# A two-layer graph network on one core: index tables, carry rows, vector features and the third pass laid out anew

## The chip, the cores and the metric

The kernel runs on 1 core of one Trainium2 chip. The metric is device time in microseconds (us), the median of several runs.

## The reference

There are 100,000 nodes with 160 features each (64 scalars and 32 three-vectors), and 25,000 edges, sorted by destination, with 4 and 8 attributes. Two layers run one after the other, each on the layer-normed and clipped rows:

```python
h = jnp.maximum(_layernorm(x), 0.0)
# layer 0, with attr = node_vec1, ys = edge_attr_4[:, :1], yv = edge_attr_4[:, 1:]
weight = silu(edge_attr_8 @ fc_w1 / sqrt(8)) @ fc_w2 / sqrt(64)          # E x 192
f_s, f_v = linear(h) * attr ; gs, gv = f_s[src], f_v[src]
m0a = gs * ys * w1_                      ; m0b = sum(gv * yv) * INV3 * w4_
m1a = gs[..., None] * yv * w2_[..., None] ; m1b = gv * ys * w3_
mid = segment_sum([m0a, m0b, m1a, m1b], dst) / 4
angle = 0.1 * mid_s @ lin3_w / sqrt(96) * attr
x = x + cos(angle) * (h @ sc_w * attr) + sin(angle) * (mid @ lin2_w * attr)
# layer 1: s, v of the new h at src; e0, e1 the edge attributes
out0 = C0 * (s * e0 @ W1 + dot(v, e1) * INV3 @ W2)
out1 = C1 * ((s @ W3) * e1 * INV3 + (v * e0) @ W4 * INV3 + cross(v, e1) @ W5 * INV6)
x = x + relu(segment_sum([out0, out1], dst) @ [Ws, Wv])
```

## The kernel before

All arithmetic is float32. Edges are cut into T = 196 tiles of 128, four tiles to a quad (Q = 49 quads); nodes are cut into U = 98 units of 1024 rows (8 rows a partition). Each engine runs its own list, written out by hand, with semaphores between them; there is no planner. The stages, in order:

- **Prologue.** SyncE (SP) loads the index tables, weights and first node rows. VectorE (DVE) makes from them the gather index `t_gat`, the scatter index `t_put` (far out of bounds where the next edge has the same destination) and keys `f_key`, and SP stores these in DRAM tables `src_tab`, `dst_tab`, `put_tab`, `key_tab`, `row_tab` (lines 409 to 418). Behind these stores in SP's list come the 13 groups of the edge network: load `scalars_t` (`net_load`, line 427), two products on TensorE (PE, line 1037), Silu on ScalarE (ACT, line 803), store `hid_tab` (line 433).
- **Pass 1.** A step is one dense unit and two edge tiles; two steps are a quad. Dense part: moments, centring (`hb`, `hr`), transposes (line 976), products (`dense_mm`, lines 981, 982), `dense_x1` (DVE, line 1358), second norm (`nmr`, line 1211), `dense_h1` (ACT, line 774, four instructions for half a unit), and the sum `yo` on GpSimd (POOL, line 649). Edge part: gather rows (`p1_gather`), transposes, products (lines 981, 982, 1066), `p1_source` (ACT, line 824, scales the product into `g_e`), `p1_features` in three DVE parts (lines 1423, 1428, 1432), transposes (line 1090), message parts (lines 1052 to 1055), message (line 1411), and the running segment sum: `same` selector times messages plus `carry` selector times the tile before (lines 1078, 1080), copied out by `p1_total` (ACT, line 832). One PE turn ("slot") is: `dense_mm`, `p1_feat_t`, `p1_parts`, `p1_source`, `p1_sum`, then `dense_tr`. `dense_tr` waits for `e_tot`, the signal of `p1_total`, as the sum and the transposed rest share PSUM bank 1. ACT's turn is `p1_feat_t`, `p1_rest`, `p1_source`, `p1_total`, then the dense copies and `dense_h1`.
- **Pass 2.** For each quad, rows at the destinations are gathered (POOL, line 606), the first layer is finished with the sums, and h of layer 1 is scattered (POOL, line 612).
- **Pass 3.** For each tile n: gather (line 738), `p3_features` (DVE, lines 1686, 1688: the row scaled by e0, and 288 products), four transposes, copy `fT` (ACT, line 951), `p3_parts` (five products, lines 1166 to 1170), `p3_message` and `p3_message_sum` (DVE, lines 1697, 1703), `p3_sum` (PE), `p3_total` (ACT), `p3_out` (DVE, line 1712), scatter (line 612). PE's slot n is `p3_tr(n-1)`, `p3_sum(n-4)`, `p3_parts(n-2)`. The selectors are built per quad from `q_row`, a row of 512 destinations that SP broadcasts to 128 partitions, in SP's list behind the load of `i_put`, which waits for the scatters of the quad two before.

Of the kernel before, what the change touches and what calls it, by code (L numbers as in the profile page):

```python
# [34 lines left out]
W_WS, W_WVK, W_WV, W_WVA, W_WVB, W_END = 2211, 2275, 2371, 2403, 2499, 2595  # L35
# [39 lines left out]
def gnn_kernel(nc, xa, src, dst, number, edges_in, scalars_in, scalars_t_in, wpack, out):  # L75
# [34 lines left out]
    row_q = row_tab.rearrange("(q c) p -> q (c p)", c=GQ)  # L110
    ed_q = edges.rearrange("p (q c) f -> q p (c f)", c=GQ)
# [9 lines left out]
    with ExitStack() as ctx:  # L121
# [32 lines left out]
        f_key = sb("f_key", [P, Q, 2 * GQ])  # L154
        t_row = two("t_row", [P, P])
# [25 lines left out]
        inv1, inv2 = four("inv1", [P, GD]), two("inv2", [P, GD])  # L181
# [11 lines left out]
        i_put = two("i_put", [P, GQ], i32)  # L193
        q_key = two("q_key", [P, 2 * GQ])
        q_row = two("q_row", [P, GQ * P])
# [10 lines left out]
        g_e = two("g_e", [P, D])  # L206
        feat = two("feat", [P, 512])
        fT = two("fT", [P, 512])
# [4 lines left out]
        n_sct = [t[0:GQ * SW, 0:CH] for t in yo]  # L213
# [55 lines left out]
        d_mm = sem("dense_product_done")  # L269
        d_scl = sem("dense_scale_ready")  # L270
# [21 lines left out]
        e_fm = sem("p1_feature_step")  # L292
# [40 lines left out]
        m_ft = sem("p3_features_ready")  # L333
        m_ss = sem("p3_scalars_copied")
# [32 lines left out]
        def _(sp):  # L367
            sp.dma_start(t_src[:, :], src).then_inc(s_tab_in, 16)
            sp.dma_start(t_dst[:, :], dst).then_inc(s_tab_in, 16)
            sp.dma_start(wp[:, :], wpack).then_inc(s_w, 16)  # L370

            sp.wait_ge(s_fill, 2)
            sp.dma_start(t_next[0:P - 1, :], dst[1:P, :]).then_inc(s_tab_in, 16)
            sp.dma_start(t_next[P - 1:P, 0:T - 1], dst[0:1, 1:T]).then_inc(s_tab_in, 16)
            sp.dma_start(t_prev[P - 1:P, 1:T], dst[P - 1:P, 0:T - 1]).then_inc(s_tab_in, 16)
# [3 lines left out]
            sp.dma_start(scalars_t.rearrange("q f p -> (q f) p"), scalars_t_in.rearrange("q f p -> (q f) p")).then_inc(s_rows, 16)  # L379
            sp.wait_ge(s_flag, 1)  # L380
            with sp.If(sp.value_load(unsorted[0:1, 0:1], min_val=0, max_val=1) > 0):

                sp.wait_ge(s_rows, 32)
# [12 lines left out]
                sp.dma_start(t_src[:, :], src_sorted).then_inc(k_tab, 16)  # L396
# [9 lines left out]
                sp.wait_ge(k_sct2, 16 * T)  # L406

            sp.wait_ge(s_tabc, 6)
            sp.dma_start(src_tab.rearrange("q p c -> p q c"), t_src[:, :].rearrange("p (q c) -> p q c", c=GQ)).then_inc(s_tab_out, 16)
            sp.dma_start(dst_tab.rearrange("q p c -> p q c"), t_gat[:, :].rearrange("p (q c) -> p q c", c=GQ)).then_inc(s_tab_out, 16)  # L410
            sp.dma_start(put_tab.rearrange("q p c -> p q c"), t_put[:, :].rearrange("p (q c) -> p q c", c=GQ)).then_inc(s_tab_out, 16)
            sp.dma_start(key_tab.rearrange("q p c -> p q c"), f_key[:, :, :]).then_inc(s_tab_out, 16)
            sp.wait_ge(s_rowsb, 1)
            sp.dma_start(row_tab[0:TA, :], t_row[0][0:TA, :]).then_inc(s_tab_out, 16)
# [1409 lines left out]
```

## Time and profile before

| | before |
|---|---|
| median of 3 runs | 2458.61 us (2458.08 to 2460.48) |
| the profiled execution's own time | 2459.89 us |
| its span, first to last instruction | 2458.1 us |
| prologue, to the end of the edge network | 0 to 111.9 us |
| pass 1 | 112 to about 1372 us |
| pass 2 | about 1376 to 1906 us |
| pass 3 | about 1907 to 2458 us |
| mean granted TensorE clock | 0.883 of full |

Busy time alone says little here: each stage has another engine that sets its pace, so each is read for itself. "Idle before" is the time an engine sat unused ahead of an instruction, with what released it. Instructions on one engine overlap at their edges, so start-to-start distances are what a turn costs.

### The profile page before, as it was taken

What the parts mean: (1) busy time and instruction counts of PE and PEld (TensorE: products, weight loads), DVE (VectorE), ACT (ScalarE), POOL (GpSimd) and SP (SyncE); (2) the same over time, 40 slices, a digit from 0 to 9 for tenths busy, and PEclk for the clock granted to TensorE, in tenths of its full rate; (3) what the DMA queues carried; (4) which work ended last, traced back from release to release, by engine and by line L of the source; (5) the groups of instructions that cost most, each with busy time, mean ns of one, the idle gap of its engine ahead of it and who ended that gap; (6) DMA issues with size and microseconds to landing.
All of it is one profiled execution on the core that took longest, in us unless ns stands there. A gap on an engine that the chain in (4) does not pass through costs nothing.

```text
span 2458.1 us, 51427 instructions
## 1 busy us (share of the span) xinstructions
PE 1824.8 (74%) x12730; PEld 1696.7 (69%) x12730; DVE 1873.4 (76%) x5982; ACT 1296.0 (53%) x3409; POOL 1477.5 (60%) x1432
## 2 busy tenths in 40 slices
PE   0788888888888888888888554544543788898887
PEld 0287778777787777877777544444443788888887
DVE  2099999999999999999999676666666566665564
ACT  0256666666666666666666555555555333333332
POOL 1045455554545555455553677777777777777776
PEclk9999999999999999999999755555555899998999
DMA  9445555555555555555555534334433334444443
GB/s 85 145 139 186 196 206 202 196 188 195 200 201 203 190 195 191 201 205 194 195 184 185 172 108 118 114 116 123 117 117 117 94 105 111 115 111 110 113 115 85
DMA packets 236558, 377.35 MB, mean 154 GB/s; under 512 B 116353, under 2 KB 146108, under 8 KB 236364
## 3 DMA queue, kind: packets, MB, share of 16 engines
q1 hardware_dynamic: 189484, 302.66, 39.1%
q0 software_dynamic: 47040, 74.31, 11.2%
q8 instruction: 12, 0.20, 0.0%
q14 instruction: 22, 0.18, 0.0%
HBM read 183.27 MB, written 201.21 MB: 156 GB/s over the span
## 4 chain that ended last, share of the span: by engine, by line
PE 33%; issue 17%; DVE 14%; ACT 12%; DMA 12%; POOL 6%; SPq 4%; ACTq 1%; DVEq 1%; POOLq 0%
ACT h L774 6%; PE bank L981 5%; DMA q_row<-row_tab 4%; PE bank L976 4%; DMA x_all<-in_xa,i_dst 3%; DVE st L1207 3%; POOL h_all L612 3%; PE bank L1090 3%; PE bank L982 3%; PE bank L1066 2%; DMA out<-yo,i_put 2%; POOL x_all L606 2%; PE bank L1158 2%; ACT h L889 2%; ACT tot L832 2%
## 5 line engine op out<-in xcount | busy, mean ns | idle before, releaser
L649 POOL TENSOR_TENSOR yo<-x,h 128x640 f32<-128x640 f32 x196 | 303.9, 1551 | 506.2 <-ACT h L774 504.9
L981 PE MATMUL bank<-wp,hT 128*128 128x160 f32 x1568 | 376.3, 322 | 0.0
L774 ACT ACTIVATE h<-x,nmr,inv 128x160 f32<-128x160 f32 x784 | 342.2, 514 | 1.5 <-DVE nmr L1211 1.5
L606 POOL DMA_INDIRECT x_e<-in_xa,i_src x192 | 210.8, 1098 | 161.1 <-issue 78.3
L981 PE MATMUL bank<-wp,eT 128*128 128x160 f32 x784 | 263.0, 428 | 51.2 <-ACT eR L897 43.7
L982 PE MATMUL bank<-wp,hR 128*128 128x64 f32 x1568 | 259.4, 247 | 0.0
L1358 DVE SCALAR_TENSOR_TENSOR x<-bank,scl,x_all 128x160 f32<-128x160 f32 x784 | 254.7, 365 | 5.1 <-PE bank L982 1.8
L982 PEld LDWEIGHTS bank<-wp,hR 128*128 128x128 f32 x1568 | 255.5, 190 | 0.0
L612 POOL DMA_INDIRECT out<-yo,i_put x196 | 209.7, 1070 | 74.3 <-issue 41.0
L612 POOL DMA_INDIRECT h_all<-h,i_put x196 | 217.4, 1109 | 59.8 <-issue 58.9
L976 PE MATMUL bank<-ident,h_e 128*128 128x128 f32 x392 | 83.9, 353 | 215.8 <-DVE hr_e L1527 215.4
L981 PEld LDWEIGHTS bank<-wp,hT 128*128 128x128 f32 x1568 | 237.7, 192 | 2.1
L738 POOL DMA_INDIRECT h<-h_all,i_src x196 | 200.2, 1022 | 61.5 <-issue 44.5
L606 POOL DMA_INDIRECT x_all<-in_xa,i_dst x196 | 192.4, 981 | 59.6 <-issue 57.8
L795 ACT ACTIVATE hT<-bank 128x512 f32<-128x512 f32 x196 | 117.0, 597 | 208.2 <-PE bank L977 208.2
L1207 DVE BATCH_NORM_STATS2 st<-x 128x6 f32<-128x320 f32 x490 | 217.9, 484 | 0.0
L976 PEld LDWEIGHTS bank<-ident,h_e 128*128 128x128 f32 x392 | 58.2, 185 | 224.7 <-DVE hr_e L1527 207.1
L981 PEld LDWEIGHTS bank<-wp,eT 128*128 128x128 f32 x784 | 163.5, 258 | 70.7 <-issue 38.2
L976 PE MATMUL bank<-ident,hb 128*128 128x128 f32 x784 | 124.3, 281 | 110.3 <-ACT tot L832 110.3
L946 ACT ACTIVATE tot<-bank 128x160 f32<-128x160 f32 x196 | 59.0, 301 | 267.9 <-PE bank L1181 264.0
L1158 PE MATMUL bank<-ident,feat 128*128 128x128 f32 x784 | 129.0, 290 | 93.2 <-DVE feat L1688 92.5
L976 PEld LDWEIGHTS bank<-ident,hb 128*128 128x128 f32 x784 | 83.1, 141 | 152.5 <-issue 137.6
(161 smaller groups left out, 5508.3 us busy)
## 6 DMA issues: line engine op xcount, KB each, us to landing
x_all<-in_xa SPq DMA_DIRECT2D x98, 644.0 KB, 5.0
h_all<-h SPq DMA_DIRECT2D x98, 640.0 KB, 3.0
out<-yo SPq DMA_DIRECT2D x98, 640.0 KB, 3.3
q_row<-row_tab SPq DMA_DIRECT2D x98, 256.0 KB
sum_tab<-tot SPq DMA_DIRECT2D x49, 322.0 KB, 4.2
y_tab<-yo SPq DMA_DIRECT2D x49, 320.0 KB
x<-y_tab SPq DMA_DIRECT2D x49, 320.0 KB
cv<-sum_tab SPq DMA_DIRECT2D x25, 322.0 KB, 3.2
```

Of the source, the lines that this page charges most:

```text
L606: nc.gpsimd.indirect_dma_start(into[:, t * width:(t + 1) * width], None, rows, bass.IndirectOffsetOnAxis(ap=index[:, t:t + 1], axis=0)).th ...
L612: nc.gpsimd.indirect_dma_start(rows, bass.IndirectOffsetOnAxis(ap=index[:, t:t + 1], axis=0), tile, None, bounds_check=N - 1, oob_is_err=F ...
L649: nc.gpsimd.tensor_tensor(yo[j][:, a:b], x1[j][:, a:b], h1[j][:, a:b], ALU.add).then_inc(d_y, 1)
L738: nc.gpsimd.indirect_dma_start(h1[j][:, t * D:(t + 1) * D], None, h1_all, bass.IndirectOffsetOnAxis(ap=i_src[j][:, t:t + 1], axis=0)).then ...
L774: ins = nc.scalar.activation(h1[j][:, k * D:(k + 1) * D], x1[j][:, k * D:(k + 1) * D], ACT.Relu, bias=nmr2[j][:, k:k + 1], scale=inv2[j][: ...
L795: nc.scalar.activation(hT[h][:, :], bank[0][:, :], ACT.Relu)
L976: nc.tensor.transpose(ps_main[:, t * P:(t + 1) * P], main[:, t * P:(t + 1) * P], ident[:, :])
L981: nc.tensor.matmul(dst_ps, main[:, t * P:(t + 1) * P], wp[:, w:w + D], start=True, stop=False)
L982: return nc.tensor.matmul(dst_ps[:, 0:DS], rest[:, :], wp[:, w + D + t * DS:w + D + (t + 1) * DS], start=False, stop=True)
L1158: ins = nc.tensor.transpose(bank[n.mod(2)][:, c * P:(c + 1) * P], feat[n.mod(2)][:, c * P:(c + 1) * P], ident[:, :])
L1207: return V.bn_stats(st[:, 2 * pair:2 * pair + 2, :].rearrange("p g k -> p (g k)"), two_rows[:, 0:D, :])
L1358: ins = V.scalar_tensor_tensor(x1[j][:, k * D:(k + 1) * D], bank[2 + pair % 2][:, k % 2 * D:(k % 2 + 1) * D], scl1[u.mod(4)][:, k:k + 1], ...
```

## The change

- **Index copies.** The four DRAM tables of indices and keys are gone. DVE copies four columns of `t_src`, `t_gat`, `t_put` from SBUF into `i_src`, `i_dst`, `i_put` some quads ahead (`index_copy`, with an address from a register); `q_key` gives way to columns of `f_dst`. `i_put` has four buffers in place of two.
- **Carry rows.** The carry selector has only its last row non-zero. A table `carry_tab` of these rows is made once (a compare of each row with the tile's predecessor), and per quad SP loads one row of 512 into partition 127 of `carry[j]`. The second `is_equal` of each quad on DVE is gone, in pass 1 and in pass 3. `row_tab` is now a copy of an input, int32.
- **Prologue.** The table stores and the transposes for rows are gone; loads are in another order; four network groups are loaded ahead in place of one; message weights take 11 products in place of 16.
- **Scale through PSUM.** `dense_inverse` writes its 8 columns into PSUM bank 2, `dense_scale` reads them there; both sit inside `dense_x1` of the unit before. PE's first product of a unit waits for the scale.
- **Vector features of pass 1.** `p1_source` on ACT writes, beside the scaled 160 columns, three more pieces of 32 columns with a stride of three, each scaled by attribute and scale (`scly`, made by one new POOL instruction per quad). `p1_features` has two DVE parts; the in-place product of line 1432 is gone. `p1_tables` moves to the even step.
- **Pass 3 in three chunks.** ACT scales the row by e0. DVE makes the 288 products into `prod`, and after `p3_message` the dot (a reduction of 96 to 32) and the cross product (64 and 32 columns). The features are 352 wide in place of 512: three transposes, four products, and a copy of `fT` in two ACT instructions. `q_row` is loaded a quad earlier, by itself.

The core of the diff:

```diff
@@ SP, pass 1 @@
             def step(v, last=False, laststore=False):
-                if v.mod(2) == 0 and (q + 1).within(Q):
-                    p1_load(q + 1)
+                if v.mod(2) == 0 and q.within(Q):
+                    p1_tables(q)
                 if v.mod(2) == 1 and q.within(Q):
-                    p1_tables(q)
+                    p1_carry(q)
                     p1_hidden(q)
+            def p1_carry(q):
+                j = q.mod(2)
+                wait(sp, e_seg, q.times(GQ, -GQ))
+                sp.dma_start(carry[j][P - 1:P, :], carry_q[q.times(1)].unsqueeze(0)).then_inc(e_ca[j], 16)
@@ SP, prologue @@
-            sp.wait_ge(s_tabc, 6)
-            sp.dma_start(src_tab.rearrange("q p c -> p q c"), ...).then_inc(s_tab_out, 16)
...
-            sp.dma_start(key_tab.rearrange("q p c -> p q c"), f_key[:, :, :]).then_inc(s_tab_out, 16)
...
+            sp.wait_ge(s_rows, 48)
-            net_load(0)
+            for g in range(4):
+                net_load(g)
+            sp.wait_ge(s_car, 1)
+            sp.dma_start(carry_tab[0:TA, :], c_row[0][0:TA, :]).then_inc(s_car_out, 16)
@@ SP, pass 3 @@
+            def p3_rows(q):
+                j = q.mod(2)
+                wait(sp, m_sc, q.times(1, -1))
+                sp.dma_start(q_row[j][:, :], row_q[q.times(1)].partition_broadcast(P)).then_inc(m_rw[j], 16)
+            def p3_step(q, ahead=True):
+                if ahead:
+                    p3_rows(q + 1)
+                p3_edges(q)
+                p3_y(q)
+                p3_carry(q)
@@ POOL @@
             def p1_scale(q):
...
+                pool.wait_ge(e_scl, q.times(4, 3))
+                pool.wait_ge(e_tb[j], q.over(2, 32, 32))
+                nc.gpsimd.tensor_tensor(scly[j][:, :].rearrange("p (t i) -> p t i", i=3), bc_last(scl_e[j][:, :], 3),
+                                        x3(q_ed[j], EW, GQ)[:, :, 1:4], ALU.mult).then_inc(e_scl, 1)
@@ ACT @@
             def p1_source(n):
-                nc.scalar.activation(g_e[n.mod(2)][:, :], bank[5 + n.mod(2)][:, 0:D], ACT.Copy,
-                                     scale=scl_e[j][:, t:t + 1]).then_inc(e_gg, 1)
+                g, b = g_e[n.mod(2)], bank[5 + n.mod(2)]
+                nc.scalar.activation(g[:, 0:D], b[:, 0:D], ACT.Copy, scale=scl_e[j][:, t:t + 1])
+                for c in range(3):
+                    ins = nc.scalar.activation(g[:, D + c:D + DV:3], b[:, DS + c:D:3], ACT.Copy,
+                                               scale=scly[j][:, 3 * t + c:3 * t + c + 1])
+                ins.then_inc(e_gg, 1)
             def p3_scalars(n):
-                nc.scalar.activation(feat[n.mod(2)][:, 448:512], h1[j][:, t * D:t * D + DS], ACT.Copy).then_inc(m_ss, 1)
+                nc.scalar.activation(f[:, 0:D], h, ACT.Copy, scale=ed(j, t, 0, 1))
+                nc.scalar.activation(f[:, 288:352], h[:, 0:DS], ACT.Copy).then_inc(m_ss, 1)
@@ PE, pass 3 @@
-                for c in range(4):
-                    ins = nc.tensor.transpose(bank[n.mod(2)][:, c * P:(c + 1) * P], ...)
+                for c in range(2):
+                    nc.tensor.transpose(b[:, c * P:(c + 1) * P], f[:, c * P:(c + 1) * P], ident[:, :])
+                nc.tensor.transpose(b[0:DV, 2 * P:3 * P], f[:, 256:352], ident[:, :]).then_inc(m_ftr, 1)
@@ DVE @@
+            def index_copy(into, table, q, signal):
+                V.tensor_copy(into[:, :], table[:, bass.ds(q.times(GQ), GQ)]).then_inc(signal, 1)
             def dense_inverse(u):
-                V.reciprocal(inv1[j][:, :], sd1[j][:, :]).then_inc(d_scl, 1)
+                V.reciprocal(bank[2][:, 2 * D:2 * D + GD], sd1[u.mod(4)][:, :]).then_inc(d_inv, 1)
             def p1_selectors(q):
-                selector(same, q.mod(2), 0)
-                selector(carry, q.mod(2), 1).then_inc(e_sc, 1)
+                selector(q).then_inc(e_sc, 1)
             def p1_features(n, part):
-                else:
-                    v.wait_ge(e_fm, n.times(1, 1))
-                    V.tensor_tensor(f[:, 224:320]..., f[:, 224:320]..., bc_mid(ed(j, t, 1, 4), DU), ALU.mult).then_inc(e_ft, 1)
             def p3_slot(n):
                 if n.within(T):
                     p3_features(n)
                 if (n - 2).within(T):
                     p3_message(n - 2)
+                if n.within(T):
+                    p3_dot_cross(n)
                 if (n - 4).within(T):
                     p3_out(n - 4)
...
-                if n.mod(4) == 0 and n.within(T):
-                    selector(carry, n.c // GQ % 2, 1).then_inc(m_sc, 1)
```

## Rows read from the trace of the kernel before

**Rows 1.** The page's slices of PE: the span in 40 equal parts.

```profile
PE   0788888888888888888888554544543788898887
```

**Rows 2.** Busy time in four stretches: PE, PEld, DVE, ACT, POOL, clock, DMA.

```profile
60.00:114.00 54.00, 45.82 (x57) 15.96 (x57) 0.00 (x0) 15.27 (x27) 0.00 (x0) 1.00 0.44 136
600.00:700.00 100.00, 83.56 (x645) 78.50 (x645) 94.68 (x271) 64.44 (x181) 52.85 (x52) 1.00 0.58 200
1700.00:1800.00 100.00, 49.29 (x193) 43.78 (x192) 67.43 (x290) 53.79 (x101) 77.75 (x74) 0.55 0.40 118
2100.00:2200.00 100.00, 86.09 (x651) 84.87 (x651) 58.58 (x198) 33.84 (x109) 76.68 (x75) 0.93 0.43 113
```

**Rows 3.** Timeline of the prologue, SP's queue and PE.

```profile
18.75 10.62 SPq L410 DMA_DIRECT2D dst_tab<-t_gat  x1
...
63.98 7.16 PE L1037 MATMUL bank<-yo,wp 32*128 32x512 f32 x8 [44.74 <-DMA yo<-scalars_t]
...
110.66 1.22 PE L1037 MATMUL bank<-yo,wp 32*128 32x128 f32 x4 [0.44 <-DMA yo<-scalars_t]
```

**Rows 4.** DMA issues: KB each, median us to landing.

```profile
scalars_t<-in_scalars_t_in SPq DMA_DIRECT2D x1, 784.0 KB, 9.7
```

**Rows 5.** Waits, 200 to 1300 us: total us, times, longest.

```profile
PE bank L976 <- ACT tot L832: 98.4, 173, 0.6
...
PE bank L1090 <- DVE feat L1432: 36.3, 43, 0.8
```

**Rows 6.** The copy at line 811, once a quad, quads 2 to 48.

```profile
L811 ACT ACTIVATE eT<-bank x47: 597/597/598, 160.5 to 1333.1; 128x512 f32<-128x512 f32 x47
```

**Rows 7.** Timeline of one turn of pass 1, ACT and PE.

```profile
608.08 0.39 ACT L824 ACTIVATE g_e<-bank,scl_e 128x160 f32<-128x160 f32 x1 [0.65 <-PE bank L1066]
608.62 0.30 ACT L832 ACTIVATE tot<-bank 128x161 f32<-128x161 f32 x1 [0.15 <-PE bank L1080]
...
609.18 0.63 PE L976 MATMUL bank<-ident,hb 128*128 128x128 f32 x4 [0.60 <-ACT tot L832]
```

**Rows 8.** ACT's groups by shape, 200 to 1300 us: busy, mean ns.

```profile
L774 ACT ACTIVATE h<-x,nmr,inv 128x160 f32<-128x160 f32 x691 | 301.7, 514 | 0.0
...
L824 ACT ACTIVATE g_e<-bank,scl_e 128x160 f32<-128x160 f32 x173 | 68.1, 394 | 112.8 <-PE bank L1066 112.8
L832 ACT ACTIVATE tot<-bank 128x161 f32<-128x161 f32 x173 | 52.8, 305 | 20.2 <-PE bank L1080 18.0
...
L817 ACT ACTIVATE xr<-bank 128x65 f32<-128x65 f32 x172 | 38.5, 224 | 18.9 <-PE bank L1055 15.4
```

**Rows 9.** Timeline, four instructions of line 774 in a row.

```profile
605.00 1.75 ACT L774 ACTIVATE h<-x,nmr,inv 128x160 f32<-128x160 f32 x4
```

**Rows 10.** Timeline, DVE beside POOL in pass 1.

```profile
606.91 1.54 POOL L649 TENSOR_TENSOR yo<-x,h 128x640 f32<-128x640 f32 x1 [4.23 <-ACT h L774]
...
607.35 1.13 DVE L1348 TENSOR_TENSOR scl<-inv,x_all 128x8 f32<-128x8 f32 x1
```

**Rows 11.** POOL's groups in pass 3 (1950 to 2430 us).

```profile
L612 POOL DMA_INDIRECT out<-yo,i_put x177 | 189.2, 1069 | 58.5 <-issue 32.4 <-DVE feat L1688 10.5 <-ACT feat L941 6.1
L738 POOL DMA_INDIRECT h<-h_all,i_src x176 | 180.1, 1023 | 53.6 <-issue 39.9 <-DVE yo L1712 8.2 <-ACT feat L941 5.5
```

**Rows 12.** Timeline of one turn of pass 3, PE and DVE.

```profile
2200.09 0.60 PE L1158 MATMUL bank<-ident,feat 128*128 128x128 f32 x4
...
2202.04 0.39 PE L1170 MATMUL bank<-msg1d,fT 128*128 128x96 f32 x2
...
2202.26 0.60 PE L1158 MATMUL bank<-ident,feat 128*128 128x128 f32 x4
...
2202.46 0.26 DVE L1697 TENSOR_TENSOR xr<-bank,q_ed 128x96 f32<-128x96 f32 x1 [0.75 <-PE bank L1170]
```

**Rows 13.** A DVE instruction on 4 columns, in pass 2.

```profile
L1571 DVE TENSOR_SCALAR trig<-trig 128x4 f32<-128x4 f32 x43 | 6.8, 158 | 0.0
```

**Rows 14.** A DVE group of pass 3, the carry selector (1950 to 2430 us).

```profile
L1384 DVE TENSOR_TENSOR carry<-q_row,q_key 128x512 f32<-128x512 f32 x44 | 29.9, 680 | 0.0
```

More of the change, by code:

```diff
@@ L192, in gnn_kernel @@
         i_dst = four("i_dst", [P, GQ], i32)
-        i_put = two("i_put", [P, GQ], i32)
-        q_key = two("q_key", [P, 2 * GQ])
-        q_row = two("q_row", [P, GQ * P])
+        scly = two("scly", [P, 3 * GQ])
+        i_put = four("i_put", [P, GQ], i32)
+        q_row = two("q_row", [P, GQ * P], i32)
         q_ed = two("q_ed", [P, GQ * EW])
@@ L205, in gnn_kernel @@
         eR = two("eR", [P, P])
[L206 removed]
+        g_e = two("g_e", [P, D + DV])
         feat = two("feat", [P, 512])
[L208 removed]
+        fT = two("fT", [P, 384])
+        prod = two("prod", [P, 3 * DV])
         xr = two("xr", [P, CW])
@@ L253, in gnn_kernel @@
         k_tab = sem("sorted_tables_loaded")
+        n_row = 64 if T > P else 32
         block = ctx.enter_context(nc.Block())
-        n_in = sem2("net_scalars_loaded")
+        n_in = [sem(f"net_scalars_loaded{i}") for i in range(4)]
         n_mm = sem("net_products_done")
@@ L509, in _ @@
                 step(At(0, v), last=v == U - 1)
-            for q in range(4):
-                p2_index(At(0, q))
             step(At(0, U + 3), laststore=True)
@@ L519, in p2_sums @@
                 sp.dma_start(cv[q.mod(4)], sum_tab[q.times(1)]).then_inc(r_cv[q.mod(4)], 16)
-            def p2_put(q):
-                j = q.mod(2)
-                wait(sp, r_put[j], q.over(2, 64))
-                sp.dma_start(i_put[j][:, :], put_tab[q.times(1)]).then_inc(r_px[j], 16)
             def p2_store(q):
@@ L632, in _ @@
                     pool.sem_inc(k_go, 1)
-                pool.wait_ge(k_tab, 80)
+                pool.wait_ge(k_tab, 64 + n_row)
+            for j in range(2):
+                nc.gpsimd.memset(carry[j][:, :], 0.0)
+            nc.gpsimd.memset(tot[1][:, :], 0.0).then_inc(s_cz, 1)
             def p1_gather(q):
                 j = q.mod(2)
-                pool.wait_ge(e_ix[j], q.over(2, 16, 16))
+                pool.wait_ge(e_ix, q.times(1, 1))
                 wait(pool, e_cen, q.times(1, -1))
+                wait(pool, e_scl, q.times(4, -4))
                 gather(xa, x_e[j], XW, i_src[j], e_g[j])
@@ L783, in dense_root1 @@
                 act.wait_ge(d_ln1, u.times(1, 1))
-                wait(act, d_scl, u.times(2, -7))
+                wait(act, d_inv, u.times(1, -3))
                 root(sd1[u.mod(4)], st1[u.mod(4)], GD, d_sq1)
@@ L1016, in dense_mm @@
                 for k in range(GQ):
+                    if h == 0 and k == 0:
+                        pe.wait_ge(d_scl, u.times(1, 1))
                     if k % 2 == 0:
@@ L1379, in dense_shift2, with selector @@
                 shift_of(nmr2[j], st2[j], inv2[j], GD, d_nmr)
-            def selector(into, j, key):
-                return V.tensor_tensor(x3(into[j], P, GQ), x3(q_row[j], P, GQ),
-                                       bc_last(q_key[j][:, key * GQ:(key + 1) * GQ], P), ALU.is_equal)
+            def selector(q):
+                j = q.mod(2)
+                key = f_dst[:, bass.ds(q.times(GQ), GQ)]
+                return V.tensor_tensor(x3(same[j], P, GQ), x3(q_row[j], P, GQ), bc_last(key, P), ALU.is_equal)
+            def index_copy(into, table, q, signal):
+                V.tensor_copy(into[:, :], table[:, bass.ds(q.times(GQ), GQ)]).then_inc(signal, 1)
             def p1_stats(q):
@@ L1486, in step @@
                     p1_message(s1 - 2)
-                if tile:
-                    p1_features(s1, 2)
                 if odd:
                     p1_selectors(q1)
+            v.wait_ge(s_src_in, 16)
+            for q in range(2):
+                index_copy(i_src[q], t_src, At(0, q, 2), e_ix)
             dense_stats(At(0, 0))
@@ L1624, in p2_step @@
                     p2_stats(q)
+                if (q + 3).within(Q):
+                    index_copy(i_dst[(q + 3).mod(4)], t_gat, q + 3, r_ix)
+                if c:
+                    wait(v, r_put[q.mod(2)], (q - 2).over(2, 64, -64))
+                    index_copy(i_put[(q - 2).mod(4)], t_put, q - 2, r_px)
                 if b:
@@ L1659, in p2_step @@
                     p2_angle(q, 7)
+            for q in range(3):
+                index_copy(i_dst[q], t_gat, At(0, q), r_ix)
             v.wait_ge(d_y, 2 * U)
```

361 lines of the change are left out of this document (174 added, 187 removed).

## The prediction

> **What bounds the kernel now.** I read the page's slices first, then the stages' busy times, then in each stage the wait that ends last. The slices show four stages: PE is 80% busy in passes 1 and 3 and half idle in pass 2 [rows 1]. The table of stretches names a different engine each time [rows 2]. From 60 to 114 us nothing but PE and ACT works; in pass 1 DVE is at 94.7%, in pass 2 POOL is at 78%, in pass 3 POOL is at 77% and PE at 86%.
>
> *Prologue.* SP stores tables until 63.98 us, where the first network product starts; the last one ends at 110.66 + 1.22 = 111.9 [rows 3]. Eight products (two groups) take 7.16 us, and 12 groups took 46.68 us, so a pair costs 7.78, of which 0.6 is waiting for a load.
>
> *Pass 1.* The quad's period is (1333.1 − 160.5)/46 = 25.49 us [rows 6]. DVE's 94.7% tempts one to call it the bound, but the waits show a loop through PE: every tile PE stands 0.57 us (98.4/173) for ACT's `tot`, and only once a quad 0.84 us (36.3/43) for DVE's features [rows 5]. Without the second the quad would be 24.65. The tail of the turn is in the timeline: `g_e` starts at 608.08, `tot` 0.54 later, PE goes on 0.56 after that [rows 7]. So what lengthens `g_e` on ACT lengthens PE's turn.
>
> *Pass 2.* PE idles half of the time and runs at 0.55 of its clock [rows 2]; POOL's indirect DMAs, eight a quad, set the pace.
>
> *Pass 3.* POOL's two groups and their idle time fill 189.2 + 180.1 + 58.5 + 53.6 = 481 of 480 us: 2.73 a tile, 10.9 a quad, most of the idle time being issue [rows 11]. PE's own turn is 2202.26 − 2200.09 = 2.17 us [rows 12]; it catches up and waits again for selectors.
>
> **The change, part by part** (profiled execution's own time 2459.9, 1.3 above the median).
>
> *Prologue, −43.* What remains before the network is the load of `scalars_t`, 9.7 us [rows 4], which landed ahead of the first store at 18.75 [rows 3]. With small transfers more (about 2) and a group load (about 3) the first product starts near 25. With four groups loaded ahead the loads vanish: 12 groups at 3.58 plus 1.22 is 44.2, end at 69, against 111.9: −43. Bounds: start at 20 gives −48; the old 7.78 a pair, or weights that come late, −35. The carry rows' compare, the clearing on POOL and the shorter weight products lie beside these 44 us, where DVE and POOL are idle [rows 2]; uncovered they would cost under 5.
>
> *Pass 1, vector features, +23.5.* ACT gains three pieces of 32 columns a tile. Two sizes of copy from PSUM, 161 columns in 0.305 and 65 in 0.224, give 0.84 ns a column; the scaled 160 took 0.394, 0.09 more than the copy [rows 8]. So a scaled piece of 32 is 0.224 − 0.028 + 0.09 = 0.285. ACT overlaps neighbours: four instructions of 0.514 took 1.75, a spacing of 0.41 for each, so 0.10 is hidden [rows 8, 9]. A piece then adds 0.18. ACT reaches `tot` after 0.29 + 3 × 0.18 = 0.84 in place of 0.54 (today 0.15 of that is waiting for PE): +0.30 a turn. The quad: 24.65 + 4 × 0.305 + 0.10 of leftover DVE waits = 25.97, +0.48, times 49 = +23.5. Bounds: pieces at 0.12 add 0.11 a turn, −15; at 0.285 with no overlap 0.60, +82.
>
> DVE loses one feature product a tile and one selector a quad, and gains the index copy, which I put between 0.158, DVE's 4-column instruction [rows 13], and 0.29: 1.3 to 3 us less a quad. That opens slack but no time, save the 0.84 wait counted above. The reciprocal into PSUM and the scale inside `dense_x1` take their old durations; the scale took 1.13 us for 8 columns while POOL was in its sum [rows 10]. With one SBUF operand it may shed that stall, which now runs into `hb` instead or disappears. Both lie in DVE's slack. `dense_mm` waits for the scale, but the scale precedes it by most of a step; if late, PE's first product of a unit waits. POOL's new 12-column product waits for the edge table and queues ahead of the later sums; POOL is 53% busy [rows 2], so nothing.
>
> Here the Trainium skill speaks against the index copies ("SBUF — State Buffer", § SBUF: two separate sides): a DVE copy of float32 within SBUF takes the port pair that GpSimd needs to write its DMA descriptors, and one side waits whole. By it 98 copies in passes 2 and 3 would cost up to about 0.2 us each, +20 by my estimate; the 1.13 us row agrees that the two engines meet, but no row here shows a copy beside an indirect DMA.
>
> *Index copies, pass 2, +3.* SP's loads were hidden, so removing them gives nothing; two copies a quad on DVE (67% busy) sit beside POOL, the bound. At 0.03 net each, 49 × 2 × 0.03 = +3; bounds 0 and, if each held POOL for 0.2 us, +20. The four `i_put` buffers remove no wait that shows.
>
> *Pass 3, +5.* The carry selector, 0.68 us on DVE a quad [rows 14], goes; beside POOL's DMAs I count 0.4 of it as gain, so POOL would want 10.5 a quad. But dot and cross come after the message, which waits for PE's parts. Today the transposes start 0.17 before the last product ends (2202.26 against 2202.43) [rows 12]. Afterwards they start behind message 0.26, reduction (as the 96-column message) 0.26, two subtractions between 0.158 and 0.26, 0.22 and 0.18 [rows 12, 13]: 0.92 less three overlaps of 0.10 (taken as ACT's) plus 0.07 of signals = 0.69 to 0.71. That is +0.88 on PE's turn. One transpose fewer gives 0.11, the dropped product 0.22 (2202.26 − 2202.04): 2.17 + 0.88 − 0.33 = 2.72, 10.9 a quad. PE's loop and POOL's then lie side by side, with little room to catch up: 11.0, +0.1 × 49 = +5. ACT's scaled row and split copy lie in its 34% of work [rows 2]. `q_row` loaded a quad earlier takes a wait away that would otherwise hold PE, already inside the 10.9. Bounds: POOL alone at 10.5, −20; cross at 1.05 of chain, +0.8 a quad, +40.
>
> Sum: 2459.9 − 43 + 23.5 + 3 + 5 = 2448.4; less 1.3, **2447 us**.
>
> **Rivals.** *B, the pieces are cheap.* If DVE's load was what made PE late (94.7% speaks for it, the waits against it), its 1.3 to 3 us less a quad count: the quad falls to 25.0 and pass 3 to 10.7: −43 − 24 − 10 + 3 = **2385**.
>
> *C, the other side: ACT's three pieces cost more than the prologue gives.* Place: between `g_e` and `tot`, every tile. The prologue and the rest give 35, 49 × (24.75 + 4e) − 49 × 25.49 = 35 at e = 0.363 a turn, a piece of 0.20. I work with 0.18; strided reads and writes speak for more. Without overlap, 0.605: +82 in place of +23.5, **2506**. The Trainium skill ("ScalarE: Activation LUTs", § What ACT_TABLE_LOAD costs) gives a fixed part, 0.833 ns a column and 93 ns for a pointer scale; my estimate from it is 0.213 a piece, e = 0.39, about 2463; its slope agrees with the 0.84 of the rows.
>
> *D, PE's clock.* Passes 2 and 3 show 0.55 at 49% busy and 0.93 at 86% [rows 2]. A turn of 2.72 with about 0.9 idle lies between. At 0.8 some 0.4 us a tile is added, +80: **2525**.
>
> *E, the change doesn't do what it says:* the network still starts late because its loads queue behind the carry rows or weights; then +20 to +40 on the forecast, 2480.
>
> **How the numbers follow.** The forecast has 0.48; its own range is 2425 to 2470 (bounds −15 on the pieces, +20 on the copies). B 0.19, C 0.21, D 0.07, E 0.05. About 0.2% of the median, 5 us, is what a measurement can tell. Of the forecast 0.33 is faster, 0.09 same, 0.06 slower; B is faster; of C 0.03 is same and 0.18 slower, of D and E 0.01 and 0.11. Faster 0.52, same 0.13, slower 0.35. The range of 8 in 10 cuts a tenth at either end, inside B's and C's spread: 2400 to 2498.
>
> **What would show it.** First network product near 25 us and last end near 69, else the prologue's step is wrong. The `eT` copy's period 26.0 (B: 25.0, C: above 26.2); `g_e` to `tot` 0.84; PE's wait for `tot` 0.87 a tile and none for DVE's features. Pass 2 at its old length within 5 us. In pass 3 PE idle before the transposes with DVE's cross as releaser, POOL no longer filled. Wrong would be: POOL's indirect DMAs longer than 1.07 and 1.02, or a granted clock in pass 3 under 0.9.

## Result and the profile after

The changed kernel takes 2485.35 us (median of 4 runs, 2481.81 to 2490.46) against 2458.35 for the kernel before on the same chip: ratio 1.0124, 95% interval 1.0101 to 1.0147. It is 27 us slower. The forecast, 2447, had the sign wrong; the range, 2400 to 2498, holds the time. The profiled execution took 2483.92 with a span of 2482.1.

First the stages. Each has an instruction whose first start marks its beginning: the first `eT` copy (pass 1), the first gather into `x_all` (pass 2) and the first gather into `h` (pass 3). These are rows of single lines; after the colon stand the shortest, median and longest duration in ns, then first and last start in us. Before:

```profile
L811 ACT ACTIVATE eT<-bank x49: 597/597/598, 113.6 to 1333.1; 128x512 f32<-128x512 f32 x49
L606 POOL DMA_INDIRECT x_all<-in_xa,i_dst x196: 942/967/1575, 1376.7 to 1878.2; - x196
L738 POOL DMA_INDIRECT h<-h_all,i_src x196: 942/975/1472, 1907.8 to 2428.6; - x196
```

The changed kernel, and its `tot` copy of pass 3, one a tile:

```profile
L816 ACT ACTIVATE eT<-bank x49: 597/597/597, 67.7 to 1312.3; 128x512 f32<-128x512 f32 x49
L604 POOL DMA_INDIRECT x_all<-in_xa,i_dst x196: 942/951/1638, 1357.2 to 1867.4; - x196
L743 POOL DMA_INDIRECT h<-h_all,i_src x196: 942/975/1399, 1897.5 to 2449.7; - x196
L958 ACT ACTIVATE tot<-bank x196: 303/304/308, 1915.3 to 2472.4; 128x160 f32<-128x160 f32 x196
```

Differences of these starts, and of the spans' ends, give:

| stage | before, us | after, us | measured | forecast |
|---|---|---|---|---|
| prologue (to the first `eT`) | 113.6 | 67.7 | −45.9 | −43 |
| pass 1 | 1263.1 | 1289.5 | +26.4 | +23.5 |
| pass 2 | 531.1 | 540.3 | +9.2 | +3 |
| pass 3 (to the end of the span) | 550.3 | 584.6 | +34.3 | +5 |
| sum | 2458.1 | 2482.1 | +24.0 | −11.5 |

So 29 of the 36 us by which the sum is off are in pass 3, 6 in pass 2. The same four stretches as in [rows 2] (stretch, length, then PE, PEld, DVE, ACT, POOL, clock, DMA share, GB/s):

```profile
60.00:114.00 54.00, 42.42 (x262) 36.62 (x261) 34.11 (x100) 28.19 (x86) 19.00 (x24) 1.00 0.39 125
600.00:700.00 100.00, 82.61 (x636) 77.42 (x636) 91.79 (x250) 69.65 (x224) 53.96 (x55) 1.00 0.56 194
1700.00:1800.00 100.00, 49.45 (x194) 44.28 (x194) 66.85 (x300) 53.70 (x102) 77.75 (x73) 0.53 0.38 116
2100.00:2200.00 100.00, 72.48 (x525) 66.40 (x525) 59.67 (x272) 42.04 (x175) 72.98 (x71) 1.00 0.39 109
```

The first stretch now holds work of pass 1 as well. Of the other three the last differs most: in pass 3 PE fell from 86% to 72% busy and POOL from 77% to 73%. No engine is full there, which points to a loop of waits. The prologue in the timeline, against [rows 3]: the first network product starts at 23.76, and all 52 run on without a load wait, to 65.94.

```profile
23.76 42.18 PE L1042 MATMUL bank<-yo,wp 32*128 32x512 f32 x52 [10.02 <-DMA yo<-scalars_t]
```

One turn of pass 1, ACT and PE, against [rows 7]:

```profile
605.01 0.32 ACT L841 ACTIVATE tot<-bank 128x161 f32<-128x161 f32 x1
...
605.58 0.63 PE L989 MATMUL bank<-ident,hb 128*128 128x128 f32 x4 [0.86 <-ACT tot L841]
...
611.84 0.40 ACT L830 ACTIVATE g_e<-bank,scl_e 128x160 f32<-128x160 f32 x1 [0.65 <-PE bank L1071]
612.13 0.65 ACT L832 ACTIVATE g_e<-bank,scly 128x32 f32<-128x32 f32 x3
612.64 0.33 ACT L841 ACTIVATE tot<-bank 128x161 f32<-128x161 f32 x1
```

`g_e` to `tot` is 0.80 (was 0.54), each piece adding (612.64 − 612.13)/3 = 0.17. PE's wait for `tot` is 0.88 a tile (was 0.57), as the waits of 200 to 1300 us say (total, times, longest):

```profile
PE bank L989 <- ACT tot L841: 149.1, 169, 1.0
```

PE's wait for DVE's features, 0.84 a quad in [rows 5], is gone from PE's list. The quad is (1312.3 − 139.9)/45 = 26.05 us, forecast 25.97.

One turn of pass 3, PE and DVE, against [rows 12]:

```profile
2209.51 0.44 PE L1168 MATMUL bank<-ident,feat 128*128 128x128 f32 x2 [0.80 <-DVE feat L1708]
...
2211.21 0.36 PE L1178 MATMUL bank<-msg1c,fT 96*128 96x96 f32 x2
...
2211.60 0.26 DVE L1715 TENSOR_TENSOR xr<-bank,q_ed 128x96 f32<-128x96 f32 x1 [1.32 <-PE bank L1178]
2211.78 0.24 DVE L1706 TENSOR_REDUCE feat<-prod 128x32 f32<-128x96 f32 x1
...
2212.10 0.19 DVE L1708 TENSOR_TENSOR feat<-prod 128x32 f32<-128x32 f32 x1
...
2212.35 0.44 PE L1168 MATMUL bank<-ident,feat 128*128 128x128 f32 x2 [0.78 <-DVE feat L1708]
```

This is a closed circle: products end at 2211.57, the message starts at 2211.60, the reduction and two subtractions follow, and the transposes start at 2212.35, 0.78 after the products' end. All that time PE stands. DVE stood 1.32 us just before it.

### The profile page after: what moved, and what is told of

It is laid out like the page before. It is cut to its first block and busy times, and to the rows that moved or that the text cites. A ratio compares the mean times of both kernels' runs of the same rounds, so it can differ in the third digit from the quotient of the medians.

```text
span 2482.1 us, 51663 instructions
## 1 busy us (share of the span) xinstructions
PE 1775.0 (72%) x12130; PEld 1619.9 (65%) x12130; DVE 1873.2 (75%) x6324; ACT 1426.8 (57%) x4389; POOL 1505.6 (61%) x1485
## 5 line engine op out<-in xcount | busy, mean ns | idle before, releaser
L651 POOL TENSOR_TENSOR yo<-x,h 128x640 f32<-128x640 f32 x196 | 326.7, 1667 | 499.5 <-ACT h L779 498.3
L604 POOL DMA_INDIRECT x_e<-in_xa,i_src x196 | 204.4, 1043 | 98.5 <-issue 70.0
L610 POOL DMA_INDIRECT h_all<-h,i_put x196 | 224.5, 1145 | 59.8 <-issue 59.2
L743 POOL DMA_INDIRECT h<-h_all,i_src x196 | 194.1, 991 | 61.7 <-issue 57.6
L1715 DVE TENSOR_TENSOR xr<-bank,q_ed 128x96 f32<-128x96 f32 x196 | 50.4, 257 | 233.8 <-PE bank L1178 233.8
L1168 PE MATMUL bank<-ident,feat 128*128 128x128 f32 x392 | 87.0, 304 | 180.3 <-DVE feat L1708 153.8
```

The source lines that it names most:

```text
L604: nc.gpsimd.indirect_dma_start(into[:, t * width:(t + 1) * width], None, rows, bass.IndirectOffsetOnAxis(ap=index[:, t:t + 1], axis=0)).th ...
L610: nc.gpsimd.indirect_dma_start(rows, bass.IndirectOffsetOnAxis(ap=index[:, t:t + 1], axis=0), tile, None, bounds_check=N - 1, oob_is_err=F ...
L651: nc.gpsimd.tensor_tensor(yo[j][:, a:b], x1[j][:, a:b], h1[j][:, a:b], ALU.add).then_inc(d_y, 1)
L743: nc.gpsimd.indirect_dma_start(h1[j][:, t * D:(t + 1) * D], None, h1_all, bass.IndirectOffsetOnAxis(ap=i_src[j][:, t:t + 1], axis=0)).then ...
L1168: nc.tensor.transpose(b[:, c * P:(c + 1) * P], f[:, c * P:(c + 1) * P], ident[:, :])
```

## The experiments

All edits are to the changed kernel; "quad" is the mean distance of the `eT` copies of pass 1, "turn" that of the `tot` copies of pass 3. The ratios are taken on one chip each, but the experiments ran on three chips, on which the kernel before took 2456.3, 2454.6 and 2453.1 against 2458.35 above. So a difference in us between two kernels is good to about 5; quads and turns come from one profiled execution each.

| kernel | us | ratio to before, 95% | quad | pass 3 turn |
|---|---|---|---|---|
| before | 2458.35 | 1 | 25.49 | 2.698 |
| changed | 2485.35 | 1.0124 (1.0101 to 1.0147) | 26.05 | 2.857 |
| cross ahead of the message | 2434.79 | 0.9917 (0.9900 to 0.9933) | – | 2.626 |
| reduction twice | 2516.76 | one run | – | 3.029 |
| vector features on DVE | 2456.70 | 1.0001 (0.9992 to 1.0011) | 25.50 | – |
| the same, POOL's sum filled | 2408.11 | one run | 24.50 | – |
| POOL's sum filled alone | 2465.18 | one run | 25.74 | – |
| pieces behind the total | 2437.64 | 0.9930 (0.9913 to 0.9947) | 25.12 | – |
| one piece of 96 | 2440.43 | one run | 25.22 | – |
| cross and pieces both | 2389.49 | 0.9739 (0.9721 to 0.9756) | 25.12 | – |
| index copies twice | 2487.67 | one run | – | – |
| both, copies moved | 2375.61 | 0.9673 (0.9655 to 0.9692) | – | – |

### Pass 3: dot and cross ahead of the message

```diff
             def p3_slot(n):
                 if n.within(T):
                     p3_features(n)
+                if n.within(T):
+                    p3_dot_cross(n)
                 if (n - 2).within(T):
                     p3_message(n - 2)
-                if n.within(T):
-                    p3_dot_cross(n)
```

> Changed kernel, with the reduction and the two subtractions of pass 3 placed ahead of the message on VectorE. Theory (the three instructions, 0.69 us, sit in TensorE's turn, as they start only after the products of the tile two before): TensorE's wait of 0.8 a tile before its transposes goes, its turn falls from 2.84 to about 1.95, GpSimd is the bound at about 2.62 a tile, pass 3 ends 196 x 0.24 = 47 us sooner, total about 2438. Rival (GpSimd is the bound, held up by more VectorE instructions, the wait of TensorE only follows it): no change, 2485.

Measured: 2434.79, 50.6 us less. The turn is (2423.1 − 1911.1)/195 = 2.626:

```profile
L958 ACT ACTIVATE tot<-bank x196: 280/304/308, 1911.1 to 2423.1; 128x160 f32<-128x160 f32 x196
```

The same instructions on the same engines, in another order. In the waits of 1950 to 2400 us PE waits in 42 tiles, once a quad, where the changed kernel had 157 waits:

```profile
PE bank L1168 <- DVE feat L1708: 82.8, 42, 5.1
```

POOL's two groups of pass 3, 1950 to 2400 us, first in the changed kernel and then with the cross ahead:

```profile
L610 POOL DMA_INDIRECT out<-yo,i_put x157 | 169.4, 1079 | 79.1 <-issue 65.6 <-DVE yo L1731 13.5
L743 POOL DMA_INDIRECT h<-h_all,i_src x157 | 155.6, 991 | 47.8 <-issue 46.6 <-DVE yo L1731 1.2
```

```profile
L610 POOL DMA_INDIRECT out<-yo,i_put x169 | 176.2, 1042 | 51.5 <-issue 36.3 <-DVE feat L1708 7.0 <-ACT feat L953 4.6
L743 POOL DMA_INDIRECT h<-h_all,i_src x169 | 172.0, 1018 | 51.5 <-issue 33.6 <-DVE yo L1731 9.4 <-DVE feat L1708 7.0
```

POOL's work for a tile is the same, 1.079 + 0.991 = 2.07 against 1.042 + 1.018 = 2.06. But before each scatter it stood idle 79.1/157 = 0.50 in the changed kernel and stands 0.30 now, as before each gather; that is the gap which POOL leaves before its indirect DMAs in pass 2 too. So POOL had slack in the changed kernel, and the rival, that POOL was the bound, is out; now POOL goes without slack and PE catches up with it.

### Pass 3: the reduction done twice behind the message

```diff
                 V.tensor_reduce(f[:, D:D + DU], dot, AX.X, ALU.add)
+                V.tensor_reduce(spare[:, 0:DU], dot, AX.X, ALU.add)
```

> Changed kernel, with the reduction of pass 3 done a second time into a spare tile, behind the message. Theory (it lies in TensorE's turn whole): every turn longer by its start-to-start 0.16, pass 3 +31 us, TensorE's wait before the transposes 0.8 to 0.96. Rival (GpSimd sets the pace): under +8.

Measured: 2516.76, +31.4. The turn grew by 0.172 us ((2505.2 − 1914.6)/195 = 3.029), a reduction's start-to-start distance (2211.94 − 2211.78 = 0.16 above), and PE's wait, 1950 to 2480 us, to 163.5/174 = 0.94:

```profile
PE bank L1169 <- DVE feat L1710: 163.5, 174, 1.0
```

What is put between the message and the cross on DVE is paid in every tile. With the first run this shows the cause in pass 3 from both sides.

### Pass 1: vector features back on DVE

```diff
             def p1_source(n):
-                nc.scalar.activation(g[:, 0:D], b[:, 0:D], ACT.Copy, scale=scl_e[j][:, t:t + 1])
-                for c in range(3):
...
-                ins.then_inc(e_gg, 1)
+                nc.scalar.activation(g_e[n.mod(2)][:, 0:D], bank[5 + n.mod(2)][:, 0:D], ACT.Copy,
+                                     scale=scl_e[j][:, t:t + 1]).then_inc(e_gg, 1)
...
+                    V.tensor_tensor(f[:, 224:320].rearrange("p (u i) -> p u i", i=3),
+                                    f[:, 224:320].rearrange("p (u i) -> p u i", i=3),
+                                    bc_mid(ed(j, t, 1, 4), DU), ALU.mult).then_inc(e_ft, 1)
```

> Changed kernel, with the vector features of pass 1 on VectorE again (in-place product, three parts) and one scaled copy on ScalarE. Theory (ScalarE's three pieces lie between the scaled rows and the total, on TensorE's turn, and the selector gone from VectorE takes the 0.84 wait of a quad away): scaled rows to total 0.54, quad of pass 1 from 26.05 to 24.65 plus at most 0.5, total 2485 - 50 = 2435 (2425 to 2460). Rival (VectorE's load sets the pace, its 92% busy): quad stays at or above 25.9, no gain.

Measured: 2456.70, −28.6, and the quad (1286.9 − 139.2)/45 = 25.50: that of the kernel before, 25.49, although the carry selector is gone. The time fell in the range that I had given (2425 to 2460), but the quad met neither theory (24.65 plus at most 0.5) nor rival (25.9 or more). The waits of 200 to 1300 us say why:

```profile
PE bank L986 <- ACT tot L838: 99.6, 173, 0.6
...
PE bank L1093 <- DVE feat L1434: 34.0, 43, 0.8
```

The wait for `tot` is back at 0.58, but the wait for DVE's features is 0.79 a quad, as in [rows 5], where I had expected it gone. DVE's freed time went into longer instructions: the centring `hb` takes 1.651 where it took 1.214 before, the in-place product 0.671 for 0.564 (means over the stretch). Hence the next two kernels.

### Pass 1: POOL's sum filled in place of computed

```diff
-                    nc.gpsimd.tensor_tensor(yo[j][:, a:b], x1[j][:, a:b], h1[j][:, a:b], ALU.add).then_inc(d_y, 1)
+                    nc.gpsimd.tensor_tensor(yo[j][:, a:a + 1], x1[j][:, a:a + 1], h1[j][:, a:a + 1], ALU.add)
+                    nc.gpsimd.memset(yo[j][:, a + 1:b], 0.0).then_inc(d_y, 1)
```

On the kernel with the features on DVE:

> The kernel with the vector features of pass 1 on VectorE again, with GpSimd's sum of pass 1 left out but for one column of 640 (the rest of the tile is filled with zero, so the output is not that of the reference). Theory (VectorE's two-operand instructions wait behind GpSimd's sum, and the 0.8 wait of TensorE for features a quad comes of that, so it stayed when the selector went): the centring back from 1.65 to 1.21 us, the in-place product from 0.67 to under 0.3, the wait for features gone, quad from 25.50 to 24.7. Rival (VectorE's order alone makes the features late): durations shorter, wait and quad as they were.

Measured: 2408.11, the quad (1239.1 − 136.8)/45 = 24.50, the wait for features gone. DVE's groups by shape, 200 to 1250 us:

```profile
L1337 DVE TENSOR_TENSOR hb<-x_all,st 128x1024 f32<-128x1024 f32 x86 | 104.3, 1213 | 0.0
...
L1435 DVE TENSOR_TENSOR feat<-feat,q_ed 128x96 f32<-128x96 f32 x172 | 42.5, 247 | 0.0
```

And on the changed kernel itself:

> Changed kernel (vector features on ScalarE), with GpSimd's sum of pass 1 left out but for one column of 640 and the rest filled with zero, so the output is not that of the reference. Theory (in the changed kernel pass 1 goes by TensorE's turn through ScalarE's pieces, and VectorE's stalls lie in slack): the centring and the selector fall to 1.21 and 0.68 us, VectorE is under 85% busy, and the quad stays at 26.0, total 2483. Rival (VectorE's stalls set the pace): quad under 25.3, total under 2450.

Measured: 2465.18, the quad (1297.4 − 138.9)/45 = 25.74. The durations fell as expected (`hb` 1.210, selector 0.682, DVE 82% busy), but the quad fell by 0.31 where I had expected no change, and stayed above the rival's 25.3. So neither was right: of 26.05, 24.50 is PE's turn without the pieces, 4 × 0.31 = 1.24 the pieces, and 0.31 is still DVE's stalls. Where these 0.31 sit the trace shows in part. PE's wait for `tot` is 0.88 in both, but in the changed kernel the weight loads ahead of the feature transposes (PEld) wait for DVE's features, a wait that the filled kernel does not have:

```profile
PEld bank L1096 <- DVE feat L1432: 5.2, 22, 0.2
```

That is 0.12 a quad; the rest was not found. The fill also makes POOL's step shorter (0.19 and 0.63 us in place of 1.54), and these runs do not separate that from what the fill no longer reads.

### Pass 1: where the pieces stand, and how many

```diff
             def slot(u, h):
...
                 if s.within(T):
                     p1_source(s)
                 if (s - 3).within(T):
                     p1_total(s - 3)
+                if s.within(T):
+                    p1_pieces(s)
```

> Changed kernel, with ScalarE's three pieces placed behind the copy of the total. Theory: TensorE's wait for the total falls from 0.87 to 0.57, as before the change; VectorE gets the pieces 0.3 us later, which its slack takes, or partly: quad 26.05 to 24.9, total about 2430. Rival (VectorE's load, with the later start, makes the features late): wait for the total short, but a new wait of TensorE for VectorE's features, quad 25.5 or more.

Measured: 2437.64, −47.7; the quad (1268.9 − 138.6)/45 = 25.12. The wait for `tot` is 101.0/175 = 0.58, and a short wait for DVE's features is there, 0.32 a quad:

```profile
PE bank L995 <- ACT tot L845: 101.0, 175, 0.6
...
PE bank L1102 <- DVE feat L1438: 13.9, 43, 0.4
```

One contiguous piece in place of three (with one scale for all of it, so the vector features are not those of the reference):

```diff
-                for c in range(3):
-                    ins = nc.scalar.activation(g[:, D + c:D + DV:3], b[:, DS + c:D:3], ACT.Copy,
-                                               scale=scly[j][:, 3 * t + c:3 * t + c + 1])
+                ins = nc.scalar.activation(g[:, D:D + DV], b[:, DS:D], ACT.Copy, scale=scly[j][:, 3 * t:3 * t + 1])
```

> Changed kernel, with ScalarE's three strided pieces of 32 columns in pass 1 made one contiguous piece of 96 columns with one scale (the vector features are then not those of the reference). Theory (a piece costs mostly its fixed part, 0.17 start to start): scaled rows to total from 0.80 to 0.54 or so, quad of pass 1 from 26.05 to about 25.0, total about 2433. Rival (the columns or the strides of the pieces cost, not their number): scaled rows to total stays above 0.70, total above 2465.

Measured: 2440.43, the quad 25.22. In the timeline the piece of 96 columns adds 0.25, from 607.61 to 607.86, and `g_e` to `tot` is 0.54:

```profile
607.32 0.39 ACT L830 ACTIVATE g_e<-bank,scl_e 128x160 f32<-128x160 f32 x1 [0.65 <-PE bank L1069]
607.61 0.33 ACT L831 ACTIVATE g_e<-bank,scly 128x96 f32<-128x96 f32 x1
607.86 0.30 ACT L839 ACTIVATE tot<-bank 128x161 f32<-128x161 f32 x1
```

The same columns in one instruction cost half of 0.51. A piece is mostly its fixed part; whether the stride adds to it was not separated.

### Both reorderings

> Changed kernel, with the dot and cross ahead of the message in pass 3 and ScalarE's pieces behind the copy of the total in pass 1, together. Theory (two waits of TensorE in two passes, independent): both gains add, 2485 - 50.6 - 47.7 = 2387 (2380 to 2395). Rival (one gain is partly the same, for example what is left of pass 1 ends in a later start of pass 3): above 2400.

Measured: 2389.49. The gains add: 50.6 + 47.7 of 2485.35 gives 2387.

### Pass 2: the index copies

```diff
                     index_copy(i_dst[(q + 3).mod(4)], t_gat, q + 3, r_ix)
+                    V.tensor_copy(spare[:, 0:GQ], t_gat[:, bass.ds((q + 3).times(GQ), GQ)])
...
                     index_copy(i_put[(q - 2).mod(4)], t_put, q - 2, r_px)
+                    V.tensor_copy(spare[:, GQ:2 * GQ], t_put[:, bass.ds((q - 2).times(GQ), GQ)])
```

> Changed kernel, with each index copy of pass 2 made a second time into a spare tile, so four on VectorE a quad in place of two. Theory (a copy holds GpSimd's writing of descriptors, so the two copies a quad are what made pass 2 9 us longer): pass 2 from 540 to 549, GpSimd's scatter and gather means longer by 0.02 to 0.05 together. Rival (the copies only shift VectorE's longer two-operand instructions to another place beside the DMAs): pass 2 between 536 and 544.

Measured: 2487.67, pass 2 from 1357.5 to 1898.4, 540.9 against 540.3 (one run of each). The theory wanted 549 and falls: the copies by themselves cost nothing that shows. What remains is their place in DVE's order. In the changed kernel DVE's centring starts 0.07 before a scatter of POOL:

```profile
1650.09 0.15 DVE L1393 COPY i_dst<-t_gat 128x4 int32 x1
...
1650.43 0.68 DVE L1525 TENSOR_TENSOR h_e<-x_all,st_e 128x512 f32<-128x512 f32 x1
1650.50 1.69 POOL L610 DMA_INDIRECT h_all<-h,i_put  x1 [0.30 <-issue]
```

With both reorderings I then put the copies behind the centring:

```diff
-                if (q + 3).within(Q):
-                    index_copy(i_dst[(q + 3).mod(4)], t_gat, q + 3, r_ix)
-                if c:
-                    wait(v, r_put[q.mod(2)], (q - 2).over(2, 64, -64))
-                    index_copy(i_put[(q - 2).mod(4)], t_put, q - 2, r_px)
                 if b:
                     p2_scales(q - 1, 0)
                 if a:
                     p2_centre(q)
+                if (q + 3).within(Q):
+                    index_copy(i_dst[(q + 3).mod(4)], t_gat, q + 3, r_ix)
+                if c:
+                    wait(v, r_put[q.mod(2)], (q - 2).over(2, 64, -64))
+                    index_copy(i_put[(q - 2).mod(4)], t_put, q - 2, r_px)
```

> The kernel with both reorderings (dot and cross ahead of the message, pieces behind the total), and in pass 2 the two index copies placed behind VectorE's centring in place of ahead of it. Theory (the copies hold nobody, but delay the centring by 0.14 us, so that it and the sum behind it fall whole into one scatter of GpSimd, which then takes 1.69 us): that scatter back to about 1.5 us, scatter mean 1.17 to 1.12, pass 2 from 540 to about 531, total about 2380. Rival (the place in the quad is set by when the gathered rows land, not by the copies): pass 2 stays at 538 to 542, total 2389.

Measured: 2375.61, 3.3% faster than before. Pass 2 is 1836.5 − 1312.6 = 523.9, where the kernel with both reorderings had 538.4 and the kernel before 531.1. The centring now starts 0.32 before the scatter, which takes 1.22 here and 1.46 in the next quad:

```profile
1650.20 0.68 DVE L1531 TENSOR_TENSOR h_e<-x_all,st_e 128x512 f32<-128x512 f32 x1
1650.52 1.22 POOL L610 DMA_INDIRECT h_all<-h,i_put  x1 [0.30 <-issue]
```

POOL's groups, 1450 to 1800 us, first both reorderings and then with the copies moved:

```profile
L610 POOL DMA_INDIRECT h_all<-h,i_put x127 | 147.1, 1158 | 38.7 <-issue 38.4 <-DVE i_dst L1399 0.3
```

```profile
L610 POOL DMA_INDIRECT h_all<-h,i_put x132 | 142.7, 1081 | 40.2 <-issue 40.2
```

The mean scatter fell by 0.077, 196 of them by 15 us, which is about the 14.5. The one scatter of four beside the centring makes the difference: from 1450 to 1800 us it took 1.54 to 1.76 in all 32 quads of the changed kernel, starting 0.00 to 0.22 behind the centring, and 1.19 to 1.54 in the 33 quads here, starting 0.10 to 0.36 behind it. In either kernel the later the scatter starts behind the centring, the shorter it is: it ends about 1.76 after the centring's start in the changed kernel, and in most quads 1.54 after it here. The place of the copies decides, their cost does not. What moved the centring against the scatters in the first place, between the kernel before and the changed one, was not separated.

## Why the prediction was wrong

The step that failed is pass 3, "+0.1 × 49 = +5", which measured +34.3. The mechanism had been seen: dot and cross wait for the message and so for the products, and lie in PE's turn. But PE's turn was sized too short, at 2.72, and so it seemed to lie side by side with POOL's; in the runs it sets the pace alone. Two links were too small. (1) The block from the transposes to the end of the products: forecast 2.17 − 0.33 + 0.17 = 2.01, measured 2211.57 − 2209.51 = 2.06. (2) The chain from there to the next transposes: 0.71, measured 0.78; the durations were as taken (0.24, 0.24, 0.19 against 0.26, 0.22, 0.18), the overlaps and signals gave less. Together that is a turn of 2.84 for 2.72. The `same` selector, which DVE does in one tile of four, is no link of this circle; in this turn of 2.82 it is done 1.1 us before the message, for which DVE still waits:

```profile
2215.53 0.67 DVE L1390 TENSOR_TENSOR same<-q_row,f_dst 128x512 f32<-128x512 int32 x1
...
2217.29 0.26 DVE L1715 TENSOR_TENSOR xr<-bank,q_ed 128x96 f32<-128x96 f32 x1 [0.65 <-PE bank L1178]
...
2218.01 0.44 PE L1168 MATMUL bank<-ident,feat 128*128 128x128 f32 x2 [0.76 <-DVE feat L1708]
```

Even so the turns with the selector take 2.94 on the mean from 1960 to 2420 us and the others 2.84, and some take more (3.06 from 2203.59 to 2206.65); why is open. The mean over the pass is 2.857, in place of my 11.0/4 = 2.75: 0.107 × 196 = 21 us.

(3) The base was wrong too. I took 10.9 a quad from POOL's "filled" time [rows 11], while the kernel before did a tile in (2448.3 − 1922.1)/195 = 2.698, 10.79 a quad: 5 us more. And that sum proves nothing: work and idle time of an engine's only two groups add up to the stretch in any kernel, in the changed one to 169.4 + 155.6 + 79.1 + 47.8 = 452 of 450 us, although POOL has slack there. What tells is the idle time before one instruction: 58.5/177 = 0.33 and 53.6/176 = 0.30 before, 0.50 and 0.30 after. The last 3 of the 29 us lie at the ends of the pass.

My bound, +40, covered it. The chance did not: with two loops side by side the slower one sets the pace, so a link taken too small can move the time only up, and I gave the even point as likeliest. My own range, 2425 to 2470, missed; that the wide range holds 2485 is luck, as it reached so far only for rivals C and D, and neither came. Rival B wanted a quad of 25.0 and got 26.05; rival E wanted a late network, which came on time.

Rival D, that PE's clock falls in pass 3, is wrong: it rose (last section).

*Prologue.* Right, −45.9 for −43; the first product came at 23.76 for 25, and the groups ran without a gap.

*Pass 1.* The amount is right, 26.05 a quad for 25.97; a piece costs 0.17 for 0.18. One reason under it is wrong. I had DVE's wait of 0.84 a quad vanish because DVE sheds work. With the features back on DVE and the selector gone, the wait was 0.79. It comes of DVE's instructions with two SBUF operands standing beside POOL's sum, and shedding one selector only moved the stall. Filling the sum ended it (24.50), moving the in-place product to ACT did too. Rival C's price, over 0.36 a turn, did not come: `g_e` to `tot` grew by 0.26, and what went beyond the forecast is not ACT's doing. But the pieces' place alone was worth 48 us, which I saw as a cost and not as an order that could be otherwise.

*Scale through PSUM.* As read: the 8-column product fell from 0.644 to 0.155 us, and the stall went on to the centring (1.214 to 1.548) and the selector (0.680 to 2.057). The groups of 200 to 1300 us, before and after:

```profile
L1336 DVE TENSOR_TENSOR hb<-x_all,st 128x1024 f32<-128x1024 f32 x87 | 105.6, 1214 | 0.0
L1348 DVE TENSOR_TENSOR scl<-inv,x_all 128x8 f32<-128x8 f32 x87 | 56.0, 644 | 0.0
```

```profile
L1339 DVE TENSOR_TENSOR hb<-x_all,st 128x1024 f32<-128x1024 f32 x84 | 130.1, 1548 | 0.0
L1390 DVE TENSOR_TENSOR same<-q_row,f_dst 128x512 f32<-128x512 int32 x42 | 86.4, 2057 | 0.0
L1350 DVE TENSOR_TENSOR scl<-bank,x_all 128x8 f32<-128x8 f32 x85 | 13.2, 155 | 0.0
```

*Pass 2.* +9.2 for +3: the copies' own cost, which I had summed, is nil by the doubled copies; their place shifts the centring against POOL's scatters. I had bounded it by +20 and named the wrong mechanism. The 98 copies that I gave to passes 2 and 3 are those of pass 2 alone; pass 3 has as many.

## What to carry to other kernels

Where no engine is full in a stage, draw the circle of waits (here products, message, transposes) and ask of each instruction moved whether it lies behind the last arrival of that circle; the same three instructions cost 50 us more behind it than ahead of it. The same holds for a copy that another engine waits for: let it go ahead of work that nobody waits for (ACT's total before its pieces, 48 us). Work taken off an engine that stalls behind another one need not come back as time; here the stall moved to the next instruction that could take it. And an engine's work and idle time always add up to the stretch; whether it is the bound shows in the idle time before one instruction.

## What the runs showed of the hardware

A DVE instruction with two SBUF operands and a POOL instruction that reads SBUF exclude one another whole. In the changed kernel:

```profile
596.69 1.54 POOL L651 TENSOR_TENSOR yo<-x,h 128x640 f32<-128x640 f32 x1 [4.73 <-ACT h L779]
596.82 2.49 DVE L1339 TENSOR_TENSOR hb<-x_all,st 128x1024 f32<-128x1024 f32 x1
```

`hb` takes 1.21 undisturbed; here it takes 2.49 and ends at 599.31, 1.08 after the sum's end at 598.23. So it goes for 22 of the 84 from 200 to 1300 us. At 205.65 DVE starts first, and it is the sum that takes 2.58, ending 1.39 after `hb`:

```profile
205.65 1.22 DVE L1339 TENSOR_TENSOR hb<-x_all,st 128x1024 f32<-128x1024 f32 x1
205.68 2.58 POOL L651 TENSOR_TENSOR yo<-x,h 128x640 f32<-128x640 f32 x1 [4.59 <-ACT h L779]
```

With the sum replaced by a fill, every `hb` takes 1.20 to 1.23. The Trainium skill says so ("SBUF — State Buffer", § SBUF: two separate sides: an exclusive lock for the whole instruction, not a split of bandwidth), and the rows agree. The same section warns that a float32 copy within SBUF keeps GpSimd from writing descriptors; here twice as many copies of four columns made a pass of 540 us 0.6 longer, so at this size no cost could be seen. But these copies are of int32, so the page's own case did not come up.

The granted clock in pass 3, 2100 to 2200 us, was 0.93 before, with PE 86% busy and waits of up to 4.6 us; 1.00 after, with PE 72% busy and a wait of 0.8 in every tile; 0.90 with the cross ahead of the message, PE 82% busy and waits of up to 5.1. The least busy PE of the three had the highest clock, but the one at 82% had a lower one than that at 86%, so the busy share alone does not put them in order.
